# Expert stage: the up weights of each tile copied inside SBUF to a ring of four and used as the standing operand, the Silu's rows no longer turned

## The reference, cut to what matters

```python
h = silu(einsum('td,edf->etf', xf, W_up))     # W_up [64, 256, 128]
y = einsum('etf,efd->etd', h, W_down)         # W_down [64, 128, 256]
routed = einsum('etd,te->td', y, cw)          # cw: 8 experts of 64 per token, the others 0
out = x + tanh(g) * (shared + routed)
```

## Time and profile before

| what | us |
|---|---|
| median of 3 runs (2924.99 to 2930.1) | 2927.0 |
| span of the profiled execution | 2561.4 |
| its own time beside the span | not given; a median run has 365.6 outside this span |
| first load of rows to last scatter, within the span | 2079.3 to 2472.4 |
| TensorE busy, whole span | 2366.4 (92%) |
| VectorE, ScalarE, GpSimd busy | 1692.1, 1525.4, 729.2 |

### The profile page before, as it was taken

How to read it: one execution, slowest core, us unless ns; L and a number is a source line. 1 busy time by engine, 2 the same in 40 slices (tenths; PEclk the granted TensorE clock), 3 DMA queues, 4 the chain that set the end, 5 groups by cost and what they waited for, 6 DMA issues and landing times. The chain is left out here.

```text
span 2561.4 us, 63498 instructions
## 1 busy us (share of the span) xinstructions
PE 2366.4 (92%) x20058; PEld 1795.7 (70%) x20059; DVE 1692.1 (66%) x5327; ACT 1525.4 (60%) x4611; POOL 729.2 (28%) x863
## 2 busy tenths in 40 slices
PE   7999999999998999999999999999999869999950
PEld 5777777777776566666666666666666658888840
DVE  4776776777674567767667767766776645555559
ACT  3777777777773656656666666665665425545530
POOL 2000000000000023322322332332332347777740
PEclk8999999999999999999999999999999989999975
DMA  5111111111113211111111111111110366666659
GB/s 155 44 36 48 46 36 48 45 42 42 45 35 95 72 30 47 42 35 41 42 40 37 42 44 32 47 42 30 47 42 28 110 211 187 186 186 188 188 186 380
DMA packets 145288, 210.06 MB, mean 82 GB/s; under 512 B 23976, under 2 KB 108506, under 8 KB 145026
## 3 DMA queue, kind: packets, MB, share of 16 engines
q1 hardware_dynamic: 114322, 139.92, 18.7%
q0 software_dynamic: 26544, 60.21, 7.0%
q10 hardware_dynamic: 4160, 6.55, 0.7%
HBM read 118.21 MB, written 96.75 MB: 84 GB/s over the span
## 5 line engine op out<-in xcount | busy, mean ns | idle before, releaser
L1454 ACT ACTIVATE wup<-bank,nmax 112x375 f32<-112x375 f32 x512 | 297.3, 585 | 127.2 <-DVE nmax L1558 126.0
L766 ACT ACTIVATE prob<-bank,nmax 112x375 f32<-112x375 f32 x512 | 293.6, 586 | 55.7 <-DVE nmax L850 51.6
L850 DVE TENSOR_REDUCE nmax<-bank 112x1 f32<-112x375 f32 x512 | 255.4, 541 | 90.2 <-PE bank L588 90.2
L2045 POOL DMA_INDIRECT expert_results<-res,dest x288 | 280.2, 973 | 118.5 <-ACT res L2163 67.0
L1558 DVE TENSOR_REDUCE nmax<-bank 112x1 f32<-112x375 f32 x512 | 255.4, 541 | 36.0 <-PE bank L1250 36.0
L1895 POOL DMA_INDIRECT expert_rows<-rows,ids x248 | 237.2, 957 | 78.6 <-issue 69.0
L2163 ACT ACTIVATE res<-bank,xr 128x256 f32<-128x256 f32 x288 | 136.4, 474 | 190.7 <-PE bank L2077 189.6
L1868 POOL TENSOR_TENSOR stats<-stats,neg_half 112x1 f32<-112x1 f32 x64 | 35.7, 557 | 654.6 <-DVE stats L1589 652.2
L1313 PE MATMUL bank<-wup,wk 128*128 128x375 f32 x512 | 219.8, 512 | 2.1 <-DMA wup<-context_turned 0.9
L1019 POOL TENSOR_TENSOR stats<-stats,neg_half 112x1 f32<-112x1 f32 x64 | 35.1, 549 | 633.7 <-DVE stats L880 629.7
L1460 ACT COPY pT<-bank 128x336 f32<-128x336 f32 x512 | 201.1, 449 | 19.7 <-PE bank L1257 19.1
(11 more groups left out here) (255 smaller groups left out, 5001.6 us busy)
## 6 DMA issues: line engine op xcount, KB each, us to landing
xr<-expert_rows SPq DMA_DIRECT2D x288, 129.0 KB
wup<-expert_results SPq DMA_DIRECT2D x14, 1024.0 KB, 18.8
wdn<-expert_results SPq DMA_DIRECT2D x14, 1024.0 KB, 20.2
wdn<-in_L_ffn_W_down_dram SPq DMA_DIRECT2D x8, 1024.0 KB, 12.2
expert_rows<-nowhere SPq DMA_DIRECT2D x56, 129.0 KB, 3.1
x_and_h_in<-stage SPq DMA_DIRECT2D x32, 224.0 KB, 2.6
xt<-x_and_h_in SPq DMA_DIRECT2D x32, 224.0 KB, 2.8
context_turned<-ctxT SPq DMA_DIRECT2D x32, 187.5 KB, 2.3
```

The source lines that it names most:

```text
L766: nc.scalar.activation(prob[:, n % RING, :NK], s_bank[r][:NQ, :NK], ACT.Exp, bias=nmax[:, r:r + 1], accum_out=rsum[:, par, h:h + 1]).then_ ...
L850: nc.vector.tensor_reduce(nmax[:, r:r + 1], s_bank[r][:NQ, :NK], AX, ALU.max, negate=True).then_inc(maxed, 1)
L1454: nc.scalar.activation(prob[:, n % RING, :NK], s_bank[r][:NQ, :NK], ACT.Exp, bias=nmax[:, r:r + 1], accum_out=rsum[:, par, n:n + 1]).then_ ...
L2045: nc.gpsimd.indirect_dma_start(results_d, bass.IndirectOffsetOnAxis(ap=dest[:, n % DEST:n % DEST + 1], axis=0), res[:, n % RES, :], None, ...
```

## The change

SyncE gets a second job per tile, `load_w`: it reads the expert from the table, waits until `up` of tile n-4 is done, and issues a DMA of 128 x 1024 bytes from `wup` to slot n mod 4 of `w_now`, inside SBUF. In the loop it stands behind `load` of the tile four ahead. `up` takes `w_now` as the standing operand, with an address known when the program is built, and streams `xrT`; its output has the hidden units on partitions, so ScalarE writes `hidT` directly. `turn_hidden` and `keep_hT` are gone; `dest` is made in `keep_xT`, ahead of the copy. `down` and `keep_result` come one tile earlier, n-1 instead of n-2, and TensorE reads the table once per tile, right before `down`. `hidT` and `w_now` lie in the room of `wo1`.

```diff
+        WR = 4
+        hidT, w_now = in_wo([P, 2, P]), in_wo([P, WR, D])
...
+                def load_w(n, b):
+                    e = from_table(mybir.EngineType.SP, n, 0, E - 1)
+                    wait(sp, upped, n - WR + 1)
+                    sp.dma_start(w_now[:, b % WR, :], wup[:, bass.ds(e, 1), :].rearrange("p o f -> p (o f)")).then_inc(w_in[b % WR], 16)
+
                 for b in range(TURN):
                     load(b, b)
+                    if b >= 4:
+                        load_w(b - 4, b - 4)
...
                 with nc.sync.Fori(1, N // TURN) as m:
                     for b in range(TURN):
                         load(m * TURN + b, b)
+                        load_w(m * TURN + b - 4, (b - 4) % TURN)
+                for n in range(N - 4, N):
+                    load_w(n, n % TURN)
...
-                def up(n, b, e):
+                def up(n, b):
                     pe.wait_ge(xT_out, n + 1)
+                    pe.wait_ge(w_in[b % WR], passes(n, b, WR) + 16)
                     for c in range(CC):
-                        mm = pe.matmul(bank[2 + b % 2][:, :P], xrT[:, b % 2, c * P:(c + 1) * P],
-                                       wup[:, bass.ds(e, 1), c * P:(c + 1) * P].rearrange("p o f -> p (o f)"),
+                        mm = pe.matmul(bank[2 + b % 2][:, :P], w_now[:, b % WR, c * P:(c + 1) * P], xrT[:, b % 2, c * P:(c + 1) * P],
                                        start=(c == 0), stop=(c == CC - 1))
...
-                def turn_hidden(n, b):
-                    pe.wait_ge(silued, n + 1)
-                    pe.transpose(bank[4 + b % 2][:, :P], hid[:, b % 2, :], ident[:]).then_inc(h_turned, 1)
...
                     for b in range(TURN):
                         n = base + b
                         if inside(n + 2):
                             turn_rows(n + 2, (b + 2) % RB)
-                        if inside(n - 2):
-                            down(n - 2, (b - 2) % RB, expert(b - 2))
+                        if inside(n - 1):
+                            down(n - 1, (b - 1) % RB, from_table(mybir.EngineType.PE, n - 1, 0, E - 1))
                         if inside(n + 1):
-                            up(n + 1, (b + 1) % RB, expert(b + 1))
-                        turn_hidden(n, b % RB)
+                            up(n + 1, (b + 1) % RB)
...
                     dve.wait_ge(x_turned, n + 1)
+                    nc.vector.tensor_tensor(dest[:, b % DEST:b % DEST + 1], xr[:, b % RB, D:D + 1], beyond[:, bass.ds(n, 1)], ALU.add)
                     nc.vector.tensor_copy(xrT[:, b % 2, :], bank[b % 2][:, :D]).then_inc(xT_out, 1)
-                def keep_hT(n, b):
-                    dve.wait_ge(h_turned, n + 1)
-                    nc.vector.tensor_tensor(dest[:, b:b + 1], xr[:, b % RB, D:D + 1], beyond[:, bass.ds(n, 1)], ALU.add)
-                    nc.vector.tensor_copy(hidT[:, b % 2, :], bank[4 + b % 2][:, :P]).then_inc(hT_out, 1)
...
-                    nc.scalar.activation(hid[:, b % 2, :], bank[2 + b % 2][:, :P], ACT.Silu).then_inc(silued, 1)
+                    nc.scalar.activation(hidT[:, b % 2, :], bank[2 + b % 2][:, :P], ACT.Silu).then_inc(silued, 1)
```

More of the change, by code:

```diff
@@ L1942, in _, with expert_phase @@
                 pool.wait_ge(scattered, 16 * TOP_K * NB)
-def expert_phase(nc, t, w, bank, rows_d, results_d, x3_d, out, table, beyond, hid, wup, wdn):
+def expert_phase(nc, t, w, bank, rows_d, results_d, x3_d, out, table, beyond, wup, wdn):
     NB, NQ, D = t["x"].shape
@@ L1968, in expert_phase @@
         xr, xrT = sb("xr", [P, RB, D + 2]), sb("xrT", [P, 2, D])
-        hidT = sb("hidT", [P, 2, P])
+        WR = 4
+        in_wo = pieces(w["wo1"])
+        hidT, w_now = in_wo([P, 2, P]), in_wo([P, WR, D])
         res = sb("res", [P, RES, D])
@@ L1973, in expert_phase @@
         x_turned, xT_out, upped, silued = sem("x_turned"), sem("xT_out"), sem("upped"), sem("silued")
-        h_turned, hT_out, downed, res_made = sem("h_turned"), sem("hT_out"), sem("downed"), sem("res_made")
+        downed, res_made = sem("downed"), sem("res_made")
+        w_in = [sem(f"weights_in{b}") for b in range(WR)]
         dest = es.enter_context(nc.sbuf_tensor("dest", [P, DEST], U32))
@@ L2058, in turn_rows, with down @@
                     mm.then_inc(x_turned, 1)
-                def up(n, b, e):
+                def up(n, b):
                     pe.wait_ge(xT_out, n + 1)
+                    pe.wait_ge(w_in[b % WR], passes(n, b, WR) + 16)
                     for c in range(CC):
-                        mm = pe.matmul(bank[2 + b % 2][:, :P], xrT[:, b % 2, c * P:(c + 1) * P],
-                                       wup[:, bass.ds(e, 1), c * P:(c + 1) * P].rearrange("p o f -> p (o f)"),
+                        mm = pe.matmul(bank[2 + b % 2][:, :P], w_now[:, b % WR, c * P:(c + 1) * P], xrT[:, b % 2, c * P:(c + 1) * P],
                                        start=(c == 0), stop=(c == CC - 1))
                     mm.then_inc(upped, 1)
-                def turn_hidden(n, b):
+                def down(n, b, e):
                     pe.wait_ge(silued, n + 1)
-                    pe.transpose(bank[4 + b % 2][:, :P], hid[:, b % 2, :], ident[:]).then_inc(h_turned, 1)
-                def down(n, b, e):
-                    pe.wait_ge(hT_out, n + 1)
                     pe.matmul(bank[6 + b % 2][:, :D], hidT[:, b % 2, :], wdn[:, bass.ds(e, 1), :].rearrange("p o d -> p (o d)"),
@@ L2080, in round @@
                 def round(base):
[L2083 to L2088, removed]
                     for b in range(TURN):
                         n = base + b
-                        if inside(n + 1):
-                            expert(b + 1)
-                        if inside(n - 2):
-                            expert(b - 2)
                         if inside(n + 2):
                             turn_rows(n + 2, (b + 2) % RB)
-                        if inside(n - 2):
-                            down(n - 2, (b - 2) % RB, expert(b - 2))
+                        if inside(n - 1):
+                            down(n - 1, (b - 1) % RB, from_table(mybir.EngineType.PE, n - 1, 0, E - 1))
                         if inside(n + 1):
-                            up(n + 1, (b + 1) % RB, expert(b + 1))
-                        turn_hidden(n, b % RB)
+                            up(n + 1, (b + 1) % RB)
                 for _ in range(20):
@@ L2107, in _ @@
                 turn_rows(1, 1)
-                up(0, 0, from_table(mybir.EngineType.PE, 0, 0, E - 1))
+                up(0, 0)
                 round(0)
@@ L2112, in _ @@
                 round(N - TURN)
-                for n in (N - 2, N - 1):
-                    pe.wait_ge(res_made, n - 1)
-                    down(n, n % RB, from_table(mybir.EngineType.PE, n, 0, E - 1))
+                pe.wait_ge(res_made, N - 2)
+                down(N - 1, (N - 1) % RB, from_table(mybir.EngineType.PE, N - 1, 0, E - 1))
             @block.vector
@@ L2134, in body @@
                     if inside(n + 2):
-                        keep_xT(n + 2, b)
-                    keep_hT(n, b)
+                        keep_xT(n + 2, b + 2)
                 tiles(body)(nc.vector)
@@ L2167, in body @@
                 def body(n, b):
-                    if inside(n - 2):
-                        keep_result(n - 2, (b - 2) % RB)
+                    if inside(n - 1):
+                        keep_result(n - 1, (b - 1) % RB)
                     if inside(n + 1):
@@ L2173, in _ @@
                 tiles(body)(nc.scalar)
-                keep_result(N - 2, RB - 2)
                 keep_result(N - 1, RB - 1)
@@ L2214, in build_kernel @@
             table = in_wq([1, table_d.shape[0] * 2]).bitcast(I32)
-            beyond, hid = in_wq([P, table_d.shape[0]]), in_wq([P, 2, P])
+            beyond = in_wq([P, table_d.shape[0]])
             layer1_phase(nc, t, w, bank, x1pre_d, ctxT_d, rows_d, x3_d, wdn, wup, table_d, table, beyond, in_wq)
-            expert_phase(nc, t, w, bank, rows_d, results_d, x3_d, out, table, beyond, hid, wup, wdn)
+            expert_phase(nc, t, w, bank, rows_d, results_d, x3_d, out, table, beyond, wup, wdn)
 _INS = ['x', 'ctx_512', 'g_xattn', 'g_ffn', 'L0_xattn_Wq', 'L0_xattn_bq', 'L0_xattn_Wk', 'L0_xattn_bk', 'L0_xattn_Wv',
```

## The result

The changed kernel takes 3037.7 us (median of 4 runs, 3036.3 to 3043.6) against 2926.0 for the kernel before: a ratio of 1.038, 95% interval 1.0366 to 1.0395, or 112 us more. The forecast was slower, 3110 us within 3070 to 3190.

A forecast was written before the change was run, and what follows sets the result against it. It took TensorE and GpSimd to pace the kernel before, and SyncE's queue the changed one at 1.99 us a tile: loop +180, straight part +7, end -4, total +183 on 2927, so 3110 us, range 3070 to 3190.

The forecast's parts named there:

- The baseline: Whole kernel before: profiled span 2561.4 us plus 366 us around it that the change doesn't touch; pace about 1.31 a tile.
- the last rival: SyncE's queue: load_w hides wholly in its room of 0.40 us a tile; 2910 to 2927 us, chance 0.04.
- The pace of the queue: SyncE in the expert stage: two issues of 0.97 us bound each tile at 1.97 with loop turns, taken as 1.99.
- the straight part: Code ahead of the loop of loads: 12 added issues of weights at 0.80 us, taken as +7, between +5 and +15.
- The round trip: From one result through loads, landing and up to a later down: 5.84 us over three tiles, 1.95 a tile.
- two near limits: Expert stage: limits at 1.95 and 1.97 us a tile, each with scatter, rarely give the smaller, so 1.99.
- What it removes: TensorE loses one turning, 0.11 us a tile (1.21 to 1.10), and VectorE a 284 ns copy; none of this decides.
- GpSimd's 1.28 a tile: Scatters stand behind TensorE: with the rest free the stage falls at most from 384 to 367, a gain of 17 us.
- Late landings: Rival: weights land in 3.5 us instead of 2.3, giving 2.34 a tile and 3205 us; chance 0.14.
- The clock: Rival: TensorE's clock falls to half, 2.3 us a tile, about 3200 us if it lasts; chance 0.07.
- The quicker queue: Rival: SyncE's register work overlaps, two issues cost 1.60 us, pace 1.84 a tile, 3070 us; chance 0.05.
- Not slower: Rival: load_w costs no more than SyncE's room of 0.40 us; 2910 to 2927, say 2920 us; chance 0.04.

The follow-up runs named there:

- b1: The kernel before with no edit, profiled once more: 2926.0 us, ratio 1.0007, span 2923.7.
- c3: Changed kernel with a weight ring of 8 and load_w(n) right behind load(n): 3041.2 us against 2940.0 for the kernel before, ratio 1.0337.
- c2: Changed kernel where load_w takes a constant expert, without table read or register work: 2997.4 us, ratio 1.0186 against the kernel before.
- d5: Changed kernel with VectorE copying the weights into the ring and ScalarE storing plainly instead of GpSimd's scatter: 2759.2 us, ratio 0.9427 against the kernel before.
- c1: Changed kernel with VectorE copying the weights into the ring instead of SyncE's DMA: 2924.6 us against 2940.0 for the kernel before, ratio 0.994.
- d1: Changed kernel with GpSimd's scatter replaced by ScalarE's plain store: 3047.9 us against 2928.4 for the kernel before, ratio 1.041.
- d2: Changed kernel where load_w moves a sixteenth of the bytes with the same number of descriptors: 3021.8 us, ratio 1.0322 against the kernel before.
- c4: Kernel before with GpSimd's indirect DMA replaced by a plain store from ScalarE's queue: 2801.0 us against 2940.0, ratio 0.9524.
- e1: Kernel before with GpSimd storing plainly by a direct DMA per tile instead of scattering: 2808.3 us, ratio 0.9553.

## Why the prediction was wrong

**The baseline is the step that failed.** The prediction says that 366 us lie around the span "if this execution is like the median run", and that the change doesn't touch them. It was not like it. Of the 362 us, 243 lie ahead of the stage (2322.6 against 2079.3 at the first load), which the change indeed leaves alone, but 119 lie in the expert stage itself: 512 us, 1.75 us a tile in 2360 to 2830 (268 tiles in 470), not 393 and 1.31. There engines wait for late signals, and SyncE with them (its waits in b1, 2360 to 2830, 470 us):

```profile
SPq L2015 <- ACT res L2163: 127.6, 102, 3.7
```

An added job in its queue first fills the room there: 1.75 - 0.97 = 0.78 us a tile, where the rows gave 1.31 - 0.97 = 0.34. Of the 0.78 the profile shows 127.6 / 268 = 0.48 as waits; the rest it doesn't explain. The prediction also misread its own row: 85.2 us over 268 loads are 0.32 us a tile, and 0.40 is the mean of one of the 211 waits. The sum doesn't use it, only the last rival does. The sum put 183 us on top of 393; the real stage started from 512. The signs were there to read: a time 366 us above the span, for which no view showed any work before or after it.

**The pace of the queue: right mechanism, a term a little small.** Forecast 1.99 us a tile, measured 2.12 on average and 2.00 as the median. The usual step is 1.98 against the forecast's 1.94. In it load_w takes 1.98 - 0.95 = 1.03 instead of 0.97, with 0.95 for load: its issue keeps the queue for 492 ns (row below) where the nearest row had 333, but what comes ahead of the issue takes 0.54 instead of 0.64. The loop turns add 0.04 (forecast 0.03). The rest, 0.10 a tile, lies in steps that are longer than the usual one, and what makes them longer is not shown.

```profile
L2033 SPq DMA_DIRECT2D wo<-wup x265: 213/492/1034, 2371.1 to 2928.4; - x133
```

The forecast for the stage was 393 + 183 = 576 and 619 was measured, 43 more: 35 in the loop (2.12 - 1.99 over 272 tiles), and some 4 each in the straight part and behind the last load. Both errors together give 43 - 119 = -76, and the forecast was 3110 - 3038 = 72 too high. That the miss is not larger is luck: two errors of opposite sign.

**The round trip** does not bind the changed kernel: c3 gave it four tiles more and gained nothing. That it stands close behind the queue, as the prediction had it, agrees with c2, which stopped at 2.0 us a tile. Its 1.95 without late signals no run shows, nor the 0.02 that the forecast added for two near limits.

**What it removes.** The 0.11 for the turning agrees in size with d5's 0.10 to 0.14. That it decides little is confirmed by c1: with the scatter in place the kernel gains 0.6%, some 15 us with VectorE's lost copy, though TensorE alone has an estimated 288 x 0.11 = 32 us less to do. What stands first in front of it is not GpSimd's 1.28 a tile, as the prediction had it (c1's stage is 511 us, not 367), but the late signals that come with its scatters.

**Late landings** did not come: d1's weights land 2.0 us after their issue, and c3's lead and d2's sixteenth of the bytes change little. **The clock** held at 0.97 with TensorE busy 0.68 of the time. **The quicker queue**, two issues in 1.60 us, is refuted by the usual step of 1.98. **Not slower** asked for less than 0.40 us per load_w (0.32 by its own row); it takes 1.03. The Trainium skill's remark ("DMA: Bandwidth & Descriptors", section "Issuing engines are not separate DMA queues"), that starting a DMA is usually small beside the DMA, does not hold for this kernel: the issue of the weights keeps the queue for 0.49 us, and with its table read and registers for 1.03, beside a landing of 2.0 us in d1; and d2 shows the stage nearly blind to the bytes.

**What is shown and what is not.** That GpSimd's scatters bring the late signals is shown by c4 and e1 for the expert stage. That it is their indirect form is not separated from one rival: both runs also write the rows in order, and no run keeps the indirect form with rows in order. For layer 1 it is argued from the timeline alone. The indirect DMAs are not enough by themselves, since one execution of the kernel before had them all and no late signal; why they bring it, and why not there, stays open.

## What to carry to other kernels

Compare the span of a profile with the times before any sum. Here 1.7 us lay between them in every other run and 366 in the one that was read; such a gap means that the profiled execution may be unlike the timed ones, in its idle times above all. A DMA per tile has a price in the queue that issues it, with its table read and register work (here 1.0 us, and 1.1 to 1.2 with what slows single steps); when that queue issues one already and its room is below this, the DMA is slower than a copy by an engine that has room (VectorE's took 0.29). A saving on one engine shows only when what stands in front of it is gone: the turning was worth some 15 us behind late signals, and 28 to 40 without them and without the scatter.

## What was not expected of the hardware

- Signals between engines came late while GpSimd worked on indirect DMAs (972 ns each): 0.9 us in the case shown, with waits on such signals of up to 3.3 us in the expert stage of b1, and 6.0 us during a row of eight in layer 1. A direct DMA on GpSimd (541 ns) and one on ScalarE's queue (343 ns) brought none of it: the stage went from 512 us to 390 and 386.
- An issue from SBUF to SBUF over 128 partitions took SyncE 492 ns, with 1024 bytes a partition and with 64; one of 1032 bytes from DRAM took 333 to 342.
- The late signals cost nothing that shows where SyncE's queue is the bound: with them the changed kernel's stage is 619 us, with ScalarE's plain store 638.
